# The second graph attention in half heads of 11 tiles, with high and low products in the same accumulator columns

## The reference, cut to what matters

```
nX = (x @ W).reshape(n, NHEAD, OUT_DIM).transpose(1, 0, 2)       # 8 heads of 64
nX = a_ln * (nX - mean) / (std + EPS) + b_ln
at1 = jnp.einsum('kno,ok->kn', nX, a1)[:, :, None]
at2 = jnp.einsum('kno,ok->kn', nX, a2)[:, :, None]
kg = jax.nn.leaky_relu(at1 + at2.transpose(0, 2, 1), negative_slope=LK_ALPHA)
mg = jnp.where(mask[None, :, :], kg * graph[None, :, :], NEG_FILL)
y = jax.nn.softmax(mg, axis=-1) @ nX + nX
```

## Time and profile before

| | |
|---|---|
| median of 3 runs | 2712.24 us (2710.72 to 2714.09) |
| the profiled execution | 2715.14 us, its span 2713.4 |
| busy over the span | PE 2329.7, DVE 1942.7, ACT 1652.9, POOL 149.7 us |
| the attention | 982 to 1695 us of the span |
| mean granted clock of TensorE | 0.939 of 2.4 GHz |

### The profile page before, as it was taken

One profiled execution on the slowest core, in us unless ns is written; L12 is line 12 of the kernel. 1 busy time (PEld: TensorE's weight loads), 2 busy tenths in 40 slices (PEclk: granted clock), 3 DMA queues, 4 the chain that ended last, 5 costly groups with the idle time before them and its releaser, 6 DMA issues. The chain is left out here.

```text
span 2713.4 us, 53321 instructions
## 1 busy us (share of the span) xinstructions
PE 2329.7 (86%) x20736; PEld 1419.4 (52%) x20736; DVE 1942.7 (72%) x3349; ACT 1652.9 (61%) x2747; POOL 149.7 (6%) x124
## 2 busy tenths in 40 slices
PE   7959999999998846777676867779998989999999
PEld 4524444444444426676666767334445745555554
DVE  5759999999996647898888989573236634455674
ACT  3438888888886645777677868562124544444542
POOL 1200000000000013121211110000000000000000
PEclk9979999999999877898888989899998999999999
DMA  4133334333331730011110101501111133334441
GB/s 178 33 113 112 128 118 149 122 117 120 125 124 65 265 91 17 23 44 33 34 38 29 43 23 46 199 6 38 32 32 67 39 110 93 106 109 120 114 123 51
DMA packets 178958, 232.70 MB, mean 86 GB/s; under 512 B 92732, under 2 KB 122748, under 8 KB 174392
## 3 DMA queue, kind: packets, MB, share of 16 engines
q1 hardware_dynamic: 171400, 193.07, 22.6%
q10 hardware_dynamic: 7344, 36.77, 4.2%
HBM read 178.20 MB, written 51.47 MB: 85 GB/s over the span
## 5 line engine op out<-in xcount | busy, mean ns | idle before, releaser
L1540 ACT ACTIVATE m_above<-m_u,m_nvs 128x1024 fp8e5<-128x1024 f32 (+1 forms) x456 | 446.0, 1065 | 9.0 <-DMA m_u<-rows 7.0
L1835 PE MATMUL m_acc<-right_x_all,m_c 128*128 128x128 f16 x3872 | 262.6, 230 | 157.7 <-DVE m_c L1615 154.1
L1041 PE MATMUL m_acc<-keep_z_hi,m_p_hi 128*128 128x512 f16 x968 | 361.5, 378 | 15.4 <-DVE m_p_lo L858 12.4
L1044 PE MATMUL m_acc<-keep_z_lo,m_p_hi 128*128 128x512 f16 x924 | 349.4, 378 | 0.0
L1046 PE MATMUL m_acc<-keep_z_hi,m_p_lo 128*128 128x512 f16 x924 | 348.0, 377 | 0.0
L1835 PEld LDWEIGHTS m_acc<-right_x_all,m_c 128*128 128x128 fp8e5 x3872 | 241.9, 104 | 164.5 <-DVE m_c L1615 159.0
L1835 PE MATMUL m_acc<-right_x_all,m_b 128*128 128x128 f16 x3872 | 258.2, 228 | 61.7 <-DVE m_b L1604 49.8
L1835 PEld LDWEIGHTS m_acc<-right_x_all,m_b 128*128 128x128 fp8e5 x3872 | 237.9, 102 | 72.5 <-DVE m_b L1604 44.2
L736 ACT ACTIVATE m_p_hi<-m_pm 128x512 f16<-128x512 f32 x242 | 150.6, 622 | 83.1 <-DVE m_pm L850 80.6
L838 DVE TENSOR_TENSOR m_sc<-m_r,m_g_row 128x512 f32<-128x512 f32 x242 | 166.0, 686 | 22.7 <-DMA m_g_row<-part 16.4
L1615 DVE TENSOR_TENSOR m_c<-m_b,keep_at 128x1024 uint32<-128x1024 uint32 (+1 forms) x144 | 177.4, 1232 | 1.1
(11 more groups left out here) (397 smaller groups left out, 5262.5 us busy)
## 6 DMA issues: line engine op xcount, KB each, us to landing
edge_a_rows<-adj ACTq DMA_DIRECT2D x40, 704.0 KB, 4.2
m_at<-adjT SPq DMA_DIRECT2D x11, 1408.0 KB
m_at<-adjT SPq DMA_DIRECT2D x11, 1280.0 KB
m_u<-rows SPq DMA_DIRECT2D x16, 512.0 KB, 3.6
low<-m_lw SPq DMA_DIRECT2D x32, 256.0 KB, 4.8
at<-edge_at SPq DMA_DIRECT2D x22, 352.0 KB, 2.5
keep_at<-at ACTq DMA_DIRECT2D x11, 704.0 KB, 5.9
keep_at_first<-at SPq DMA_DIRECT2D x22, 352.0 KB, 3.0
```

The source lines that it names most:

```text
L1041: last = pe.matmul(to, hi, z_hi[:, j, of], start=(j == 0), stop=(j == T - 1), skip_group_check=True)
L1044: pe.matmul(to, hi, z_lo[:, j, of], start=False, stop=False, skip_group_check=True)
L1540: last = act.activation(above[:, q % RA, j - j0, 0:w], u[:, g % RU, 0:w], ACT.Relu, bias=nvs[:, k, j:j + 1], scale=STEEP, saturate=False)
L1835: last = pe.matmul(to, ring[:, q % RB, j, t * P:(t + 1) * P], y[k % 2][:, j0 + j, n], start=(n == 0 and ch == 0 and j == 0 and t % 2 == 0) ...
```

## The change: what it does

- A group is a head and a half of the output: 11 tiles, 1408 columns; there are 16 groups in place of 24. VectorE makes two of a group's 22 `above` rows itself, in place of three. The ring of u (the rows that `above` is made from) has two slots of 1408 in place of three of 1024.
- High and low products go into the same 64 columns of PSUM: TensorE runs two matmuls of 64 columns with the same piece of mask where it ran one of 128 (L1822 and L1824 of the new code). The low half isn't scaled by 2048 (LS) any more. `low` and `join` go, and `shrink` and `total` read PSUM themselves; `shrink` waits for TensorE's last products of its group (c_used).
- The mean: TensorE adds a head's rows with 22 float32 matmuls of a matrix of ones (`sum_column`), and VectorE writes the row in three small steps (`mean_row`, `mean_high`, `mean_rest`). `weigh` waits for no mean.
- GpSimd has two memsets left. a_ln and b_ln are applied by VectorE to the result (`stretch`, `shift`), behind `add_own`.
- The steps beside the masks are placed anew (`settle`, `prepare`, and for the last group `settle_early`), and ScalarE's `split` with them: behind chunk 5 of a head's first half and chunk 3 of its second.
- at8 in DRAM is laid out by partition, input tile and column: layer 0 stores rows of 256 bytes (before 2816), layer 2 reads such rows, layer 3 the same 128 bytes at another distance.

```diff
         def store_mask(ib, half):
             sp.wait_ge(at8_ready[half], ib + 1)
-            sp.dma_start(dram["at8"][ib, :, js(half), :], at8_pairs[:, half]).then_inc(at8_out[half], 16)
+            sp.dma_start(dram["at8"][:, js(half), ib * P:(ib + 1) * P], at8_pairs[:, half]).then_inc(at8_out[half], 16)
...
         def load_at(i):
-            act.dma_start(at8[:, i], dram["at8"][i]).then_inc(at_in, 16)
+            act.dma_start(at8[:, 2 * i:2 * i + 2], dram["at8"][:, 2 * i:2 * i + 2]).then_inc(at_in, 16)
...
-        then(dve.scalar_tensor_tensor(d1[:], d1[:], YS * LS, here_too, ALU.mult, ALU.mult))
-        then(dve.scalar_tensor_tensor(d2[:], d2[:], YS * LS, here_too, ALU.mult, ALU.mult))
-        then(dve.memset(d2[ISO:ISO + 1, :, T - 1], YS * LS))
+        then(dve.scalar_tensor_tensor(d1[:], d1[:], YS, here_too, ALU.mult, ALU.mult))
+        then(dve.scalar_tensor_tensor(d2[:], d2[:], YS, here_too, ALU.mult, ALU.mult))
...
 kit = Kit(nc, stack, "m1")
-NB, CJ = len(BLOCKS), 4
+NB, CJ = 2, 4
 CH = [(j0, min(CJ, T - j0)) for j0 in range(0, T, CJ)]
-NC, ALL = len(CH), H * len(BLOCKS)
-RA, RB, RU, RC = 3, 3, 3, 3
-WIDE, HT, NT = 4 * BW, T // 2, 8
-OWN = {0: (3,), 2: (11,), 4: (19,)}
+NC, ALL = len(CH), H * NB
+RA, RB, RU, RC = 3, 3, 2, 3
+HT, WIDE = T // 2, T // 2 * P
+OWN = {1: (6,), 4: (18,)}
...
-y = [room[:, at:at + Y].bitcast(F16).rearrange("p (t n c) -> p t n c", n=2, c=2 * DH) for at in Y_AT]
+y = [room[:, at:at + Y].bitcast(F16).rearrange("p (t n l e) -> p t n l e", n=2, l=2, e=DH) for at in Y_AT]
...
-lowp, both = (room[:, at + i * 2 * NT * DH:at + (i + 1) * 2 * NT * DH].rearrange("p (t n e) -> p t n e", n=2, e=DH) for i in range(2))
+part_c, num, ex = (room[:, at + i * HT * DH:at + (i + 1) * HT * DH].rearrange("p (t e) -> p t e", e=DH) for i in range(3))
...
-num, ex, yo, den = kit.sb("num", [NT, DH]), kit.sb("ex", [NT, DH]), kit.sb("yo", [2, NT, DH]), kit.sb("den", [NT])
-acc = kit.ps("acc", [2, 4, 512])
+yo, den = kit.sb("yo", [2, HT, DH]), kit.sb("den", [HT])
+acc, column = kit.ps("acc", [2, 3, 512]), kit.ps("column", [2, 512])
...
+def words_of(g, ch):
+    j0, nj = CH[ch]
+    return at8[:, j0:j0 + nj, (g % NB) * WIDE // 4:(g % NB + 1) * WIDE // 4]
...
-        def mean(k):
-            of = c[:, k % RC]
-            pool.wait_ge(scaled, once(k))
-            then(pool.tensor_tensor(tree[:, 0:HT], of[:, 0:HT], of[:, HT:T], ALU.add))
-            pool.partition_all_reduce(cs[:], tree[:, 0], P, RADD).then_inc(cs_made, 1)
-            pool.wait_ge(cs_made, k + 1)
-            pool.tensor_scalar(of[ISO:ISO + 1, T - 1, :], cs[ISO:ISO + 1, :], 1.0 / N, None, ALU.mult).then_inc(mean_made, 1)
...
-        def shift(k):
-            of = c[:, k % RC]
-            pool.wait_ge(yf_made, turn(k, 1))
-            pool.tensor_tensor(of, of, aln[:].unsqueeze(1).broadcast_to([P, T, DH]), ALU.mult).then_inc(stretched, 1)
-            pool.wait_ge(stretched, k + 1)
-            pool.tensor_tensor(of, of, bln[:].unsqueeze(1).broadcast_to([P, T, DH]), ALU.add).then_inc(c_made, 1)
-        pool.memset(minus[:], -1.0).then_inc(minus_made, 1)
-        for k in range(H):
-            mean(k)
-            shift(k)
+        pool.memset(minus[:], -1.0)
+        pool.memset(ones32[:], 1.0).then_inc(ones_made, 1)
...
-            act.activation(halves(y[k % 2][:, of, n])[:, :, 0], yf[:, of, :], ACT.Copy, scale=1 / LS).then_inc(yhi_made, 1)
-        def low(g):
-            nt, t0 = size(g % NB)
-            act.wait_ge(c_used, (g + 1) * NC)
-            if g > 0:
-                act.wait_ge(both_made, g)
-            act.activation(lowp[:, 0:nt], acc_view(g, nt)[:, :, :, 1], ACT.Copy, scale=1 / LS).then_inc(low_made, 1)
+            act.activation(y[k % 2][:, of, n, 0], yf[:, of, :], ACT.Copy).then_inc(yhi_made, 1)
...
                 if ch == 1 and g > 1:
                     exp(g - 2)
-                if ch == 1 and g > 0:
-                    low(g - 1)
-                if k + 1 < H and (n, ch) in ((1, 2), (2, 0)):
-                    split(k + 1, n - 1)
+                if (g, ch) == (LAST_G, 4):
+                    exp(g - 1)
+                if k + 1 < H and (n, ch) in ((0, 5), (1, 3)):
+                    split(k + 1, n)
...
-        def join(g):
-            nt, t0 = size(g % NB)
-            dve.wait_ge(low_made, g + 1)
-            dve.tensor_tensor(both[:, 0:nt], acc_view(g, nt)[:, :, :, 0], lowp[:, 0:nt], ALU.add).then_inc(both_made, 1)
...
         def shrink(g):
-            k, n = divmod(g, NB)
-            nt, t0 = size(n)
-            dve.wait_ge(both_made, g + 1)
-            dve.tensor_tensor(both[:, 0:nt, 1], both[:, 0:nt, 1], over_tiles(f2[:, k, t0:t0 + nt]), ALU.mult).then_inc(part_made, 1)
+            dve.wait_ge(c_used, (g + 1) * NC)
+            if g > 0:
+                dve.wait_ge(num_made, g)
+            dve.tensor_tensor(part_c, acc_view(g)[:, :, 1], over_tiles(f2[:, g // NB, tiles_of(g)]), ALU.mult).then_inc(part_made, 1)
         def total(g):
-            nt, t0 = size(g % NB)
             dve.wait_ge(part_made, g + 1)
-            dve.tensor_tensor(num[:, 0:nt], both[:, 0:nt, 0], both[:, 0:nt, 1], ALU.add).then_inc(num_made, 1)
+            if g > 0:
+                dve.wait_ge(yo_made, 2 * g)
+            dve.tensor_tensor(num, acc_view(g)[:, :, 0], part_c, ALU.add).then_inc(num_made, 1)
...
+        def add_own(g):
+            k = g // NB
+            dve.wait_ge(yo_made, 2 * g + 1)
+            dve.tensor_tensor(yo[:, g % 2], yo[:, g % 2], c[:, k % RC, tiles_of(g), :], ALU.add).then_inc(yo_made, 1)
...
             of = part(k, hf)
             dve.wait_ge(scaled, once(k, hf))
-            if hf == 1:
-                dve.wait_ge(mean_made, k + 1)
...
         def rest(k, n, hf=1):
             of = part(k, hf)
-            hi, lo = (halves(y[k % 2][:, of, n])[:, :, l] for l in range(2))
             dve.wait_ge(yhi_made, turn(k, n, hf))
-            dve.scalar_tensor_tensor(lo, hi, -LS, yf[:, of, :], ALU.mult, ALU.add).then_inc(ylo_made, 1)
+            dve.tensor_tensor(y[k % 2][:, of, n, 1], yf[:, of, :], y[k % 2][:, of, n, 0], ALU.subtract).then_inc(ylo_made, 1)
+        def mean_row(k):
+            dve.wait_ge(column_made, k + 1)
+            if k > 0:
+                dve.wait_ge(row_made, 3 * k)
+            dve.tensor_scalar(vrow[ISO:ISO + 1, :], column[ISO:ISO + 1, k % 2, 0:DH], YS / N, YS, ALU.mult, ALU.add).then_inc(row_made, 1)
+        def mean_high(k):
+            dve.wait_ge(row_made, 3 * k + 1)
+            dve.wait_ge(ylo_made, turn(k, 1))
+            dve.tensor_copy(y[k % 2][ISO:ISO + 1, T - 1, 1, 0], vrow[ISO:ISO + 1, :]).then_inc(row_made, 1)
+        def mean_rest(k):
+            dve.wait_ge(row_made, 3 * k + 2)
+            dve.tensor_tensor(y[k % 2][ISO:ISO + 1, T - 1, 1, 1], vrow[ISO:ISO + 1, :], y[k % 2][ISO:ISO + 1, T - 1, 1, 0],
+                              ALU.subtract).then_inc(row_made, 1)
...
+        def settle(g, ch, late):
+            if (ch, late) == (0, 1):
+                shrink(g)
...
+        def prepare(k, n, ch, late):
+            if (n, ch, late) == (0, 4, 0):
+                weigh(k, 0)
...
+        def beside(g, ch, late):
             k, n = divmod(g, NB)
+            if g == LAST_G:
+                settle_early(g - 1, ch, late)
+            elif g > 0:
+                settle(g - 1, ch, late)
+                if g > 1 and (ch, late) == (2, 1):
+                    elu(g - 2)
+            else:
+                prepare_rest_of_first(ch, late)
+            if n == 0 and k > 0 and (ch, late) == (0, 0):
+                mean_rest(k)
             if k + 1 < H:
+                prepare(k + 1, n, ch, late)
...
         def products(g, ch, n, ring):
-            k = g // NB
-            i0, nb = BLOCKS[g % NB]
             j0, nj = CH[ch]
             q = g * NC + ch
-            for t in range(2 * nb):
-                to = acc[:, g % 2, t // 2, (t % 2) * 256 + n * P:(t % 2) * 256 + (n + 1) * P]
+            of = y[(g // NB) % 2]
+            for t in range(HT):
+                to = acc[:, g % 2, t // 4, (t % 4) * P + n * DH:(t % 4) * P + (n + 1) * DH]
                 for j in range(nj):
-                    last = pe.matmul(to, ring[:, q % RB, j, t * P:(t + 1) * P], y[k % 2][:, j0 + j, n],
-                                     start=(n == 0 and ch == 0 and j == 0 and t % 2 == 0), stop=(ch == NC - 1 and j == nj - 1),
+                    mask = ring[:, q % RB, j, t * P:(t + 1) * P]
+                    pe.matmul(to, mask, of[:, j0 + j, n, 0], start=(n == 0 and ch == 0 and j == 0 and t % 4 == 0), stop=False,
+                              skip_group_check=True)
+                    last = pe.matmul(to, mask, of[:, j0 + j, n, 1], start=False, stop=(ch == NC - 1 and j == nj - 1),
                                      skip_group_check=True)
             return last
+        def sum_column(k):
+            pe.wait_ge(scaled, once(k))
+            pe.wait_ge(ones_made, 1)
+            if k >= 2:
```

(22 more changed lines are left out.)

286 lines of the change are left out of this document (128 added, 158 removed).

## The result

The changed kernel takes 2534.68 us (median of 4 runs, 2533.49 to 2536.37), the kernel before on the same chip 2711.48 (2707.63 to 2714.09): 0.9349 of the time, with a 95% interval of 0.9333 to 0.9366, or 177 us less. The forecast was 2528, with 2503 to 2585 as its range.

The account below looks back on a forecast made before the run. VectorE bounds the second attention outside its waits for GpSimd, and the waits bound the rest. 478 + 16.5 + 24 + 10 = 528.5 us there, 184.5 less; 2715.1 becomes 2530.6, forecast as a 2528 median, range 2503 to 2585.

Parts of the forecast that it names:

- The waits for GpSimd: Second attention: VectorE stands idle 104.3 us in `weigh` for GpSimd's mean, 87.9 in seven heads and 16.4 in the first.
- its slowing of VectorE: Second attention: VectorE's instructions run longer beside GpSimd's `shift`, 51.6 us of busy time over three groups of instructions.
- VectorE's busy time: Second attention after the change: instruction durations of 517.5 us, less 39.5 for overlapping starts, leave 478 us, against 592.2 before.
- the overlap: On VectorE each instruction starts 0.09 us before the one ahead ends; 465 instructions take off 39.5 us.
- rival C: TensorE pays a price per narrow matmul, so 64 columns don't cost half; slower than before, 2902 us; chance 5%.
- The column sums: TensorE's 176 float32 matmuls at 0.11 us each, 19 us, standing where it waits for a new group's first mask.
- New wait 1: VectorE waits for ScalarE's comparisons held behind `split`: 2.8 us in seven heads, 20, plus 4 in group 0.
- rival B: ScalarE never regains its lead; VectorE waits a whole chunk, 5.5 us, at both halves, 82 in all: 2576 us; chance 10%.
- Rival A: TensorE's clock stays at 0.85 in the second attention, its 473 us become 556: 2572 us in all; chance 13%.
- New wait 2: `shrink` on VectorE waits for TensorE's last products of the group: forecast hidden; if bare, 3 us x 15 = 45.
- my own sign: The prediction called itself wrong if, among other signs, `shrink` waited over 1 us per group.
- The margin of 10 us: Second attention: 10 us added, as a choice, for what three even engines cost each other beyond the named waits.

Follow-up runs that it names:

- both edits above: Changed kernel without the column sums and mean rows, and with ScalarE's first split of the next head one chunk later: 2506.12 us, 0.9216 of the kernel before.
- spread: Changed kernel with the bulk loads of c and of the first x and y rows in pieces one chunk apart: 2526.71 us, 0.9335 of the kernel before.

## Why the prediction was right

**The waits for GpSimd** (104.3) and **its slowing of VectorE** (51.6) were read rightly, the second too low by 17. Alone they bring 172 us of the 177. The new blocks and `settle` steps bring 35 more (stretch 541.6 without GpSimd, 507.0 with both edits above, though VectorE has taken over the scale and shift in between), and the column sums with the mean rows and the place of the split give 30.5 back. Both of these figures come from copies that leave out the mean; no run keeps the old blocks of 8, 8 and 6 tiles and moves only GpSimd's two parts to other engines, so what the half heads are worth in a whole kernel is not shown.

**VectorE's busy time**: 486.5 against 478 (the row above, which ends at 1518.00, has 485.6; the last `elu` ends at 1518.90). The durations were right (514.1 us summed, 517.5 forecast). The step that failed is the overlap, 0.09 us an instruction, read in a quiet stretch. Over 467 starts it came to 27.6 us, not 39.5: 340 instructions start 0.081 us before the end of the one ahead, but 105 start behind that end (0.05 us on the mean), and 22 come behind a longer wait.

**ScalarE**: 473.5 against 473, the comparison 1.455 against 1.46.

**TensorE**: the 64-column product at 29.3 ns was right, and rival C is out. By the Trainium skill (TensorE: Matmul & The Clock Gate, Back-to-back issue gap) streams of products with their weights keep 81 ns at 128 columns; the trace disagrees, with 56 ns, and my estimate of 54 ns for 64 columns, which came from the 81, stands against 29 measured. (The prediction also calls 54 ns the part of 81 that isn't columns. That part is 81 - 53.3 = 27.7; 54 is the whole price that follows for 64 columns, 26.7 + 27.7.) The column sums were the mis-sized term: 40.8 us (8 x 5.10) where I took 0.11 each, 19 in all; 0.23 is above even my upper bound of twice 0.11. The rows that I took the 0.11 from the earlier trace rows are transposes (L1207), which stand in the trace as one instruction each; a float32 product stands as two, and each of the two costs 0.116 (5.10 / 44). The sums didn't fall into a pause either, as I had supposed ("where TensorE waits for the new group's first mask anyway"): all 18.7 us that TensorE waits for a mask b in the changed kernel are two waits, 18.3 of them at the start of the stretch.

**New wait 1** was right to a tenth: 2.8 us in each head forecast, 2.81 to 2.82 measured, 21.3 with group 0 against 24. So rival B, with a whole chunk of wait at both halves of a head, is out. Rival A is out as well: the granted clock was 1.00 in the windows from 1045 to 1429.

**New wait 2** failed: forecast hidden, measured 14.4. Its reasoning ("at most chunk 5's products and a rest of chunk 4") is a count inside one group; over a head TensorE's queue doesn't run empty, because it needs 63.1 us, and a head takes 63.2 to 64.3 (from one wait for the comparisons to the next, behind a first that is 68.0). The two sources are the sums (without them the 4.6 us before 1066.23 are gone, and 14.4 becomes 8.8) and the issue gaps behind bulk transfers (spread, 15.8 becomes 7.0). By my own sign, over 1 us a group, it fell just short of wrong: 0.9 us a group on the mean, with 4.6 and 6.0 in two of them. The margin of 10 us "for what three even engines cost each other" was a choice and no reading; that it covered most of this is luck.

**Outside the stretch**: nothing, as forecast.

The sum: 478 + 16.5 + 24 + 10 = 528.5 was forecast; 486.5 + 15.3 + 21.3 + 14.4 = 537.5 was measured. The 9 us that this is more are made up in large part by the 7 us by which the rest ran shorter than in the profiled execution of before (2001.2 to 1994.2), which is chance: the mechanism was read well, and the 2528 against 2534.7 looks a little better than it was.

Not settled: why the stages outside vary by some 6 us between executions.

## What to carry to other kernels

A wait is worth what it shows only if the engine that waits is the bound and nothing stands level behind it: taking out one engine's work in a copy of the kernel (here the mean, 125 us) prices it before a redesign does. When three engines come out within 2% of each other, an edit that takes waits from one of them can give nothing (here 20 us of waits for 1.3 us); find which two share the bound and ease both in one step. Small products in float32 have a fixed price each: join their columns. And look at what the DMA engines do ahead of a pause that no engine explains, before looking for its cause in the program.
